# The value bias moved from GpSimd's additions to a row of the attention's value tail, with another order of prologue, loads and splits

## The chip, the cores and the metric

The kernel runs on one core of one Trainium2 chip. The metric is the device time of one execution in microseconds (us); smaller is better. The engines are TensorE (PE; PEld is its weight load), VectorE (DVE), ScalarE (ACT) and GpSimd (POOL). SyncE (SP) issues nearly all DMAs.

## The reference

A cross attention with layer norm and residual, and then a mixture of 16 experts and one shared expert, again with layer norm and residual, over x of 4 x 1024 x 256, a context of 4 x 154 x 256 and hidden size 128. Everything is fp32.

```python
q = einsum('bsd,de->bse', layernorm(x), Wq) + bq
k = einsum('bsd,de->bse', ctx, Wk) + bk
v = einsum('bsd,de->bse', ctx, Wv) + bv
scores = where(mask, q @ k.T / sqrt(256), -inf)
x = x + softmax(scores) @ v
...
xf = layernorm(x)
scores = sigmoid(l2norm(xf) @ l2norm(gate_w).T)
combine = top 8 of 16 scores, divided by their sum
routed = sum over e of combine_e * (silu(xf @ w_gate_e) * (xf @ w_up_e)) @ w_down_e
shared = silu(xf @ sw_gate) * (xf @ sw_up) @ sw_down
x = x + routed + shared
```

The sum of the softmax weights is one, so a bias on v reaches the attention's output as that same bias.

## The kernel before

The 4096 tokens are worked in 8 chunks of 512 (four tiles of 128; two halves q of two tiles each). Each chunk runs through 17 experts (expert 0 is the shared one), and in the places between experts the attention, layer norms and router of the next chunk are fitted in. The instructions of each engine stand in an order written by hand, and semaphores join the engines. The tables `PE_AT`, `ACT_AT`, `DVE_AT`, `POOL_AT`, `POOL_SOON` and `POOL_FIRST` say at which place s or s + .5 of the loop over experts a step of the next chunk (or, for SOON, of the chunk after it) stands.

TensorE works in three passes: each fp32 operand is split into a high and a low part, and high times high, high times low and low times high are summed (lines 393 to 395). For expert e of chunk c, written (c, e), the chain is: `gate` and `up` on PE (12 matmuls of 512 columns), `tanh_gate` on ACT (line 866), `silu_up` on DVE (lines 1145 and 1149), `weighted` on POOL (line 1351, times the routing weights in `cb`, or 1345 for the shared expert), `hidden_hi` on ACT (line 873), `hidden_lo` on DVE (line 1155), and `down` on PE (12 matmuls of 256 columns into y_ps). PE runs `gate` and `up` three experts ahead of `down`.

In chunk 0 the weights too are split, one expert at a time: a load of 384 KB into one of three staging places (`load_stage`), `split_hi` on ACT (line 795), and `split_lo` on DVE (line 999) or, for the experts in `POOL_SPLITS`, on POOL (line 1287). `load_stage(e)` waits for both splits of expert e - 3. In the loop, `split_hi(s + 5)` and `split_lo(s + 5)` stand ahead of `hidden_hi(c, s + 1)` and `hidden_lo(c, s + 1)` on their engines.

Of the 154 keys 128 are handled as one block, and 26 as a tail padded to 32 rows. The tail's values of all four batches come from one product (`value_tails`, line 484), are split into `vt`, and for batches 1 to 3 moved by nine DMAs to `Vtail` (`move_v_tails`, line 316). `ptail` holds the tails of the exponentials, `Vtail` those of the values, stacked as high, high and low in 96 rows; line 564 multiplies them. The exponentials are not normalised before: `residual` (line 1100) multiplies the product by 1 / esum and adds x. The bias bv is added to x by POOL (`add_bv`, line 1315, two instructions per chunk), and `residual` waits for it.

`mask_and_max` on DVE scales and masks the scores (line 1063), takes the maxima (1067) and negates them (1070), for the exponentials on ACT (`exps`, line 815). `add_bias` on POOL (line 1304) prepares the mask plus the query bias's part of the scores for a chunk. `write_t2_lo` (line 1050) makes the low part of the normalised tokens, for which `logits` on PE (line 575) waits.

## Time and profile before

| | us |
|---|---|
| Median of 3 runs | 651.84 |
| Lowest and highest run | 650.86, 651.99 |
| The profiled execution's own time | 650.85 |
| Its span, first to last instruction | 648.7 |
| PE busy in the span | 634.6 |
| DVE busy in the span | 472.7 |
| POOL busy in the span | 294.7 |
| ACT busy in the span | 235.7 |

The profile is one execution. PE busy counts matmuls that overlap at their ends once. What PE does not do in the span, 648.7 less 634.6, is 14.1 us. A timeline row gives the start of an instruction (or of a run of like ones, xN), how long it took, and in brackets how long its engine had been idle before it and what ended that.

### The profile page before, as it was taken

The numbers are of one execution on the slowest core, as the hardware profiler recorded it, in microseconds if no ns is written. First come the engines' busy times: TensorE is split into PE (matmuls) and PEld (weight loads), VectorE is DVE, ScalarE is ACT, GpSimd is POOL, SyncE is SP. The second block draws the span as 40 slices with busy tenths as digits, with TensorE's granted clock in tenths as the row PEclk, the third lists the DMA queues.
The fourth block names the chain that finished last, engine by engine and source line by source line (L and its number), as shares of the span: only waits on it lengthen the run. The fifth ranks groups of instructions, "written<-read, shape, count | busy, mean of one in ns | idle before, by whom it ended". The sixth has DMA issues, their size and how long they took to land.

```text
span 648.7 us, 10466 instructions
## 1 busy us (share of the span) xinstructions
PE 634.6 (98%) x3688; PEld 551.5 (85%) x3688; DVE 472.7 (73%) x941; ACT 235.7 (36%) x500; POOL 294.7 (45%) x275
## 2 busy tenths in 40 slices
PE   8898999999999999999999999999999999999997
PEld 7576888889888888888888898888888888888886
DVE  3779897868967588766868689675887768575443
ACT  5644444333243323433243332433234332432221
POOL 2517687333743356333563337433464334423333
PEclk9999899999999999999999999999999999999999
DMA  7265663424225324053244342263240531242100
GB/s 212 68 168 193 175 176 79 149 70 151 63 35 198 90 83 97 24 174 107 74 89 131 89 148 64 36 198 98 73 98 22 177 107 42 56 132 98 65 1 33
DMA packets 112655, 67.19 MB, mean 104 GB/s; under 512 B 80996, under 2 KB 102396, under 8 KB 112604
## 3 DMA queue, kind: packets, MB, share of 16 engines
q1 hardware_dynamic: 111516, 65.74, 36.0%
q10 hardware_dynamic: 1088, 0.79, 0.4%
q8 instruction: 30, 0.49, 0.3%
q14 instruction: 21, 0.17, 0.1%
HBM read 55.79 MB, written 10.42 MB: 102 GB/s over the span
## 4 chain that ended last, share of the span: by engine, by line
PE 91%; DVE 5%; issue 2%; ACT 1%; POOL 1%; POOLq 0%; ACTq 0%; DVEq 0%
PE y_ps L393 9%; PE gate_ps L395 9%; PE gate_ps L394 9%; PE up_ps L395 9%; PE up_ps L394 9%; PE gate_ps L393 9%; PE up_ps L393 9%; PE y_ps L394 9%; PE y_ps L395 9%; PE f_ps L538 2%; DVE hs L1155 1%; DVE W L999 1%; PE up_ps L402 1%; PE f_ps L575 1%; PE f_ps L393 1%
## 5 line engine op out<-in xcount | busy, mean ns | idle before, releaser
L1351 POOL TENSOR_TENSOR hidden<-hidden,cb 128x512 f32<-128x512 f32 x128 | 193.9, 1515 | 278.5 <-DVE hidden L1149 234.3
L866 ACT ACTIVATE hidden<-gate_ps 128x512 f32<-128x512 f32 x136 | 81.3, 598 | 292.9 <-PE gate_ps L395 292.9
L1145 DVE SCALAR_TENSOR_TENSOR hidden<-hidden,gate_ps 128x512 f32<-128x512 f32 x136 | 92.7, 681 | 102.9 <-ACT hidden L866 102.7
L393 PE MATMUL y_ps<-W,hs 128*128 128x256 f32 x544 | 154.7, 284 | 5.0 <-DVE hs L1155 5.0
L394 PE MATMUL y_ps<-W,hs 128*128 128x256 f32 x544 | 151.6, 279 | 0.0
L395 PE MATMUL y_ps<-W,hs 128*128 128x256 f32 x544 | 151.4, 278 | 0.0
L1155 DVE TENSOR_TENSOR hs<-hidden,hs 128x512 fp32r<-128x512 f32 x136 | 111.1, 817 | 21.8 <-ACT hs L873 21.6
L393 PEld LDWEIGHTS y_ps<-W,hs 128*128 128x128 f32 x544 | 102.2, 188 | 13.6 <-ACT hs L873 5.0
L393 PE MATMUL gate_ps<-xT,W 128*128 128x512 f32 x272 | 107.9, 397 | 0.0
L395 PE MATMUL gate_ps<-xT,W 128*128 128x512 f32 x272 | 107.6, 396 | 0.0
L394 PE MATMUL gate_ps<-xT,W 128*128 128x512 f32 x272 | 107.3, 395 | 0.0
L395 PE MATMUL up_ps<-xT,W 128*128 128x512 f32 x272 | 107.1, 394 | 0.0
L394 PE MATMUL up_ps<-xT,W 128*128 128x512 f32 x272 | 106.8, 393 | 0.0
L393 PE MATMUL up_ps<-xT,W 128*128 128x512 f32 x272 | 106.5, 392 | 0.0
L394 PEld LDWEIGHTS y_ps<-W,hs 128*128 128x128 f32 x544 | 102.7, 189 | 4.1
L1149 DVE TENSOR_TENSOR hidden<-hidden,up_ps 128x512 f32<-128x512 f32 x136 | 93.5, 688 | 12.5 <-PE up_ps L395 0.4
L395 PEld LDWEIGHTS y_ps<-W,hs 128*128 128x128 f32 x544 | 102.4, 188 | 0.0
L873 ACT ACTIVATE hs<-hidden 128x512 fp32r<-128x512 f32 x136 | 85.2, 626 | 44.2 <-POOL hidden L1351 42.1
L394 PEld LDWEIGHTS up_ps<-xT,W 128*128 128x128 f32 x272 | 51.2, 188 | 11.7
L393 PEld LDWEIGHTS up_ps<-xT,W 128*128 128x128 f32 x272 | 51.3, 188 | 11.6
L395 PEld LDWEIGHTS gate_ps<-xT,W 128*128 128x128 f32 x272 | 51.4, 189 | 10.9
L395 PEld LDWEIGHTS up_ps<-xT,W 128*128 128x128 f32 x272 | 51.3, 188 | 10.8
(162 smaller groups left out, 664.0 us busy)
## 6 DMA issues: line engine op xcount, KB each, us to landing
cb<-c_rows SPq DMA_DIRECT2D x64, 512.0 KB, 4.8
blocks<-in_x_dram SPq DMA_DIRECT2D x28, 128.0 KB, 2.9
xin<-in_x_dram SPq DMA_DIRECT2D x7, 512.0 KB, 4.1
t_rows<-blocks SPq DMA_DIRECT2D x28, 128.0 KB, 2.7
xs<-t_rows SPq DMA_DIRECT2D x7, 512.0 KB, 3.5
out_dram<-x SPq DMA_DIRECT2D x7, 512.0 KB, 6.2
p_rows<-blocks SPq DMA_DIRECT2D x28, 80.0 KB, 2.3
stage<-in_L_ffn_w_gate_dram SPq DMA_DIRECT2D x16, 128.0 KB, 2.5
```

Of the source, the lines that this page charges most:

```text
L393: mm(ps, lh, rh, start=first and i == 0, stop=False)
L394: mm(ps, lh, rl, start=False, stop=False)
L395: ins = mm(ps, ll, rh, start=False, stop=last and i == len(pairs) - 1)
L402: turn(up_ps[:, 0, 0:P], ident[:], ident[:])
L538: ins = mm(to, xs[:, k, j * P:(j + 1) * P], A[:, c // 2, k, :], start=k == 0, stop=k == KD - 1)
L575: mm(f_ps[0:2 * E, 0, :], G[:, k, :], xT[:, par, HI, k, :], start=k == 0, stop=False)
L866: af(ew[:, i, :], gate_ps[:, i, :], ACT.Tanh, scale=0.5).then_inc(tanh_done, 1)
L873: af(hs[:, i, HI, :], h[:, i, :], ACT.Copy).then_inc(h_hi, 1)
L1145: V_.scalar_tensor_tensor(out=ew[:, i, :], in0=ew[:, i, :], scalar=1.0, in1=gate_ps[:, i, :], op0=ALU.add, op1=ALU.mult).then_inc(silu_don ...
L1149: V_.tensor_tensor(ew[:, i, :], ew[:, i, :], up_ps[:, i, :], ALU.mult).then_inc(prod_done, 1)
L1155: V_.tensor_tensor(hs[:, i, LO, :], h[:, i, :], hs[:, i, HI, :].bitcast(F32), ALU.subtract) \
L1351: pg.tensor_tensor(h[:, i, :], ew[:, i, :], cb[:, pair % PLACES, (e - 1) % 2, :], ALU.mult) \
```

## The change

The bias of the values is no longer added to x. `bv_places` is a row of 128 zeros with a one at place 26 of each batch's 32, and one more matmul (one row deep, 256 columns) adds bv into row 26 of each batch's value tail in `value_tails`. ACT's exponentials put their sums no longer into `esum` of their own but into column 154 of `att`, so that the sum becomes row 26 of the exponentials' tail, and meets bv in the product of the tails: the output gets esum times bv, and bv after the division. `add_bv` and its 16 instructions on POOL are gone, with the 128 KB load for it.

The rest is order. The negation of the maxima is folded into the reduction. `add_bias` for the chunk after next goes from place 9.5 to 12.5. In the prologue both `exps` stand next to each other on ACT, the split of the tail values is divided, `router_scaled` and `turn_router` come later, `ln2(0, 1)` comes ahead of `ln2_scale(0, 0)`, and the loads of experts 3 and 4 and of the next chunk's x blocks go ahead of the nine tail DMAs, which go ahead of expert 5's load. In the loop the splits of weights stand behind `hidden_hi` and `hidden_lo`, and `split_lo(3)` ahead of the router. In the last chunk, `gate` and `up` of expert 16 come one `down` earlier.

```diff
-POOL_SOON = dict(add_bias=(9.5,), ln1_std=(11.5, 11.5), add_bv=(13.5, 14.5))
+POOL_SOON = dict(add_bias=(12.5,), ln1_std=(11.5, 11.5))
-POOL_FIRST = dict(ln1_std=(.5, .5), add_bv=(2.5, 4.5))
+POOL_FIRST = dict(ln1_std=(.5, .5))
-        bvb = sb("bvb", [P, D])
+        bv_row = sb("bv_row", [1, D])
+        bv_places = sb("bv_places", [1, B * PAD])
+        esum = att[:, :, KEYS]
...
@@ sync @@
-                sp.wait_ge(vt_split, 4)
+                sp.wait_ge(vt_split, 2)
...
+            sp.dma_start(bv_row[:], bv.partition_broadcast(1)).then_inc(bv_loaded, 16)
             sp.dma_start(wv_in, Wv.rearrange("(k p) e -> p k e", p=P)).then_inc(wv_loaded, 16)
             sp.dma_start(gw_in, gate_w).then_inc(gw_loaded, 16)
-            sp.dma_start(bvb[:], bv.partition_broadcast(P)).then_inc(bv_loaded, 16)
             for e in range(STAGES):
                 load_stage(e)
+            load_stage(STAGES)
+            load_stage(STAGES + 1)
+            load_x_blocks(1)
             move_v_tails()
-            for e in range(STAGES, STAGES + 3):
-                load_stage(e)
-            load_x_blocks(1)
             load_x(1)
+            load_stage(STAGES + 2)
             spread(0, 0)
...
@@ tensor @@
-                    ins = mm(y_ps[:, 0, D:2 * D], ctxTt[:, k, :], wv_in[:, k, :], start=k == 0, stop=k == KD - 1)
-                ins.then_inc(vt_made, 1)
+                    mm(y_ps[:, 0, D:2 * D], ctxTt[:, k, :], wv_in[:, k, :], start=k == 0, stop=False)
+                pe.wait_ge(bv_loaded, 16)
+                pe.wait_ge(pads_set, 2)
+                mm(y_ps[:, 0, D:2 * D], bv_places[:], bv_row[:], start=False, stop=True).then_inc(vt_made, 1)
...
             attend(0, 0)
-            turn_router()
             attend(0, 1)
             values(1, y_ps[:, 0, 0:D])
+            turn_router()
...
+                    if not ahead and s + AHEAD == NE - 1:
+                        gate(c, NE - 1)
+                        up(c, NE - 1)
                     down(c, s)
                     if ahead:
                         front(s, c + 1)
-                    if (s + AHEAD < NE or ahead) and not (c == 0 and s == 1):
+                    if (s + AHEAD < NE - 1 or ahead) and not (c == 0 and s == 1):
...
@@ scalar @@
                     af(att[:, j, 0:KEYS], att[:, j, 0:KEYS], ACT.Exp, bias=nmax[:, j:j + 1],
-                       accum_out=esum[:, j:j + 1]).then_inc(exped, 1)
+                       accum_out=att[:, j, KEYS:KEYS + 1]).then_inc(exped, 1)
...
             exps(0, 0)
-            write_vt_hi()
+            exps(0, 1)
+            vt_hi_first()
             write_v_hi(0, y_ps[:, 0, 0:D])
-            exps(0, 1)
             probs_hi_first(0)
             probs_hi_first(1)
+            write_vt_hi()
...
             write_v_hi(1, y_ps[:, 0, 0:D])
+            split_hi(3)
             bias_row_rest()
             router_hi()
-            split_hi(3)
+            split_hi(4)
             t2_hi_first(0)
             t2_hi_first(1)
             read_a_rest(0)
-            split_hi(4)
...
+                    if s + 1 < NE or ahead:
+                        hidden_hi(c, s + 1)
                     if c == 0 and s + EARLY < NE:
                         split_hi(s + EARLY)
-                    if s + 1 < NE or ahead:
-                        hidden_hi(c, s + 1)
...
@@ vector @@
-                V_.tensor_reduce(rsum[:, 2 * q:2 * q + 2], att[:, 2 * q:2 * q + 2, 0:KEYS], AX_X, ALU.max) \
-                    .then_inc(maxes, 1)
-                dve.wait_ge(maxes, upto(c, 2, q + 1))
-                V_.tensor_scalar(nmax[:, 2 * q:2 * q + 2], rsum[:, 2 * q:2 * q + 2], -1.0, None, ALU.mult) \
+                V_.tensor_reduce(nmax[:, 2 * q:2 * q + 2], att[:, 2 * q:2 * q + 2, 0:KEYS], AX_X, ALU.max, negate=True) \
                     .then_inc(maxed, 1)
...
-                dve.wait_ge(x_biased, upto(c, 2, q + 1))
...
             residual(0, 1)
+            ln2(0, 1)
             ln2_scale(0, 0)
-            ln2(0, 1)
             ln2_scale(0, 1)
...
             split_lo(2)
+            split_lo(3)
             sum_logits(0)
...
             hidden_lo(0, 0)
-            split_lo(3)
             write_v_lo(2, f_ps[:, 0, 0:D])
...
+                    if s + 1 < NE or ahead:
+                        hidden_lo(c, s + 1)
                     if c == 0 and s + EARLY < NE and s + EARLY not in POOL_SPLITS:
                         split_lo(s + EARLY)
-                    if s + 1 < NE or ahead:
-                        hidden_lo(c, s + 1)
...
@@ gpsimd @@
-                pg.memset(ident[:], 0.0).then_inc(pool_step, 1)
+                pg.memset(ident[:], 0.0)
+                pg.memset(bv_places[:], 0.0).then_inc(pool_step, 1)
...
-                pg.memset(att[:, :, KEYS:KROW], 0.0).then_inc(pads_set, 1)
+                pg.memset(att[:, :, KEYS + 1:KROW], 0.0).then_inc(pads_set, 1)
+                pg.memset(bv_places[:].rearrange("o (b r) -> o b r", r=PAD)[:, :, TAIL:TAIL + 1], 1.0).then_inc(pads_set, 1)
...
-            def add_bv(c, q):
-                if c == 0:
-                    pool.wait_ge(bv_loaded, 16)
-                    pool.wait_ge(t1_turned, q + 1)
-                pool.wait_ge(ln1_stats, upto(c, 2, q + 1))
-                xh = xin[:, 2 * q:2 * q + 2, :]
-                pg.tensor_tensor(xh, xh, bvb[:].unsqueeze(1).broadcast_to([P, 2, D]), ALU.add).then_inc(x_biased, 1)
```

DVE's order in the prologue, from the maxima of the first half to the tail probabilities of the first half, before (small is a tile with sums and maxima, zT here the router's weights):

```order
L1067 TENSOR_REDUCE small<-att 128x2
L1070 TENSOR_SCALAR small<-small 128x2
L1063 SCALAR_TENSOR_TENSOR att<-f_ps,small,keepb 128x154 x2
L1067 TENSOR_REDUCE small<-att 128x2
L1070 TENSOR_SCALAR small<-small 128x2
L983 TENSOR_SCALAR zT<-cb,gsq 16x256
L976 TENSOR_TENSOR Vtail<-y_ps,Vtail 32x256
L978 TENSOR_TENSOR vt<-y_ps,vt 128x256
L964 TENSOR_TENSOR V<-y_ps,V 128x256
L1076 RECIPROCAL small<-small 128x4
```

The same stretch in the changed kernel:

```order
L1085 TENSOR_REDUCE small<-att 128x2
L1081 SCALAR_TENSOR_TENSOR att<-f_ps,small,keepb 128x154 x2
L1085 TENSOR_REDUCE small<-att 128x2
L991 TENSOR_TENSOR Vtail<-y_ps,Vtail 32x256
L979 TENSOR_TENSOR V<-y_ps,V 128x256
L1090 RECIPROCAL small<-att 128x4
```

The two negations are gone, and the router's weights and the low part of vt have left this stretch for a place behind the tail probabilities.

DVE's order in chunk 0, from the low values of batch 3 to the low hidden part of expert 3, before (W<-stage is `split_lo`, hs<-hidden,hs is `hidden_lo`):

```order
L964 TENSOR_TENSOR V<-f_ps,V 128x256
L999 TENSOR_TENSOR W<-stage,W 128x768
L1155 TENSOR_TENSOR hs<-hidden,hs 128x512
...
L1063 SCALAR_TENSOR_TENSOR att<-f_ps,small,keepb 128x154 x2
L1067 TENSOR_REDUCE small<-att 128x2
L1070 TENSOR_SCALAR small<-small 128x2
L1145 SCALAR_TENSOR_TENSOR hidden<-hidden,gate_ps 128x512
L1149 TENSOR_TENSOR hidden<-hidden,up_ps 128x512
L999 TENSOR_TENSOR W<-stage,W 128x768
L1155 TENSOR_TENSOR hs<-hidden,hs 128x512
```

The same stretch in the changed kernel:

```order
L979 TENSOR_TENSOR V<-f_ps,V 128x256
L1168 TENSOR_TENSOR hs<-hidden,hs 128x512
L1017 TENSOR_TENSOR W<-stage,W 128x768
...
L1081 SCALAR_TENSOR_TENSOR att<-f_ps,small,keepb 128x154 x2
L1085 TENSOR_REDUCE small<-att 128x2
L1158 SCALAR_TENSOR_TENSOR hidden<-hidden,gate_ps 128x512
L1162 TENSOR_TENSOR hidden<-hidden,up_ps 128x512
L1168 TENSOR_TENSOR hs<-hidden,hs 128x512
L1017 TENSOR_TENSOR W<-stage,W 128x768
```

Each weight split now stands behind the hidden part that stood behind it, and the negation is gone.

POOL's order in the changed kernel in chunk 0 between the norms of the chunk after next and the shared expert of the next chunk:

```order
L1358 TENSOR_TENSOR hidden<-hidden,cb 128x512
L1320 TENSOR_TENSOR keepb<-keep,brow 128x616
L1358 TENSOR_TENSOR hidden<-hidden,cb 128x512 x3
L1352 TENSOR_SCALAR hidden<-hidden 128x512
L1358 TENSOR_TENSOR hidden<-hidden,cb 128x512 x8
```

Before, the same stretch had the two additions of bv and no keepb:

```order
L1351 TENSOR_TENSOR hidden<-hidden,cb 128x512 x2
L1315 TENSOR_TENSOR xin<-xin,bvb 128x512
L1351 TENSOR_TENSOR hidden<-hidden,cb 128x512
L1315 TENSOR_TENSOR xin<-xin,bvb 128x512
L1351 TENSOR_TENSOR hidden<-hidden,cb 128x512
L1345 TENSOR_SCALAR hidden<-hidden 128x512
L1351 TENSOR_TENSOR hidden<-hidden,cb 128x512 x8
```

keepb is `add_bias`; it now stands directly behind `weighted` of expert 13, and nothing else is left between the experts.

## Rows read from the trace of the kernel before

**Rows 1.** The page, part 1: busy time of each engine, share, instructions.

```profile
PE 634.6 (98%) x3688; PEld 551.5 (85%) x3688; DVE 472.7 (73%) x941; ACT 235.7 (36%) x500; POOL 294.7 (45%) x275
```

**Rows 2.** Timeline of PE: start, us, engine, line, operation; in brackets idle and releaser.

```profile
15.79 1.02 PE L484 MATMUL y_ps<-x,hidden 128*128 128x256 f32 x4
...
18.80 0.44 PE L545 MATMUL f_ps<-ident,att 128*128 128x128 f32 x2 [1.13 <-ACT att L815]
...
31.11 0.66 PE L508 MATMUL f_ps<-ident,xn 128*128 128x128 f32 x4 [1.06 <-DVE xn L1014]
...
33.92 0.62 PE L575 MATMUL f_ps<-xT,G 128*32 128x512 f32 x2 [0.61 <-issue]
...
56.92 0.35 PE L393 MATMUL y_ps<-W,hs 128*128 128x256 f32 x1 [1.01 <-DVE hs L1155]
...
63.44 0.36 PE L393 MATMUL y_ps<-W,hs 128*128 128x256 f32 x1 [2.06 <-DVE hs L1155]
...
96.96 0.36 PE L393 MATMUL y_ps<-W,hs 128*128 128x256 f32 x1 [0.89 <-DVE hs L1155]
```

**Rows 3.** Windows: the stretch 64 to 72 us; PEclk is the third from last.

```profile
64.00:72.00 8.00, 8.00 (x41) 6.87 (x40) 5.73 (x9) 1.85 (x3) 5.64 (x4) 0.79 0.74 191
```

**Rows 4.** Timeline of PE behind the longest gap, two neighbouring matmuls.

```profile
65.39 0.63 PE L394 MATMUL gate_ps<-xT,W 128*128 128x512 f32 x1
65.82 0.63 PE L395 MATMUL gate_ps<-xT,W 128*128 128x512 f32 x1
```

**Rows 5.** Timeline of DVE in the prologue, and one row of ACT.

```profile
15.70 0.47 DVE L1067 TENSOR_REDUCE small<-att 128x2 f32<-128x308 f32 x1
16.21 1.58 DVE L1070 TENSOR_SCALAR small<-small 128x2 f32<-128x2 f32 x1
...
30.32 0.73 DVE L1014 TENSOR_SCALAR xn<-x,meanvar,small 128x256 f32<-128x256 f32 x2 [1.11 <-POOL small L1295]
...
32.53 1.29 DVE L1044 TENSOR_TENSOR xT<-f_ps,xT 128x512 fp32r<-128x512 f32 x2 [1.05 <-ACT xT L804]
...
15.02 1.59 ACT L795 ACTIVATE W<-stage 128x768 fp32r<-128x768 f32 x2
```

**Rows 6.** Timeline of POOL: prologue, and the second expert of chunk 0.

```profile
15.96 3.58 POOL L1287 TENSOR_TENSOR W<-stage,W 128x768 fp32r<-128x768 f32 x2 [2.28 <-ACT W L795]
...
47.66 1.29 POOL L1351 TENSOR_TENSOR hidden<-hidden,cb 128x512 f32<-128x512 f32 x1 [5.33 <-DMA cb<-c_rows]
```

**Rows 7.** Timeline of DVE in chunk 0.

```profile
43.81 0.95 DVE L999 TENSOR_TENSOR W<-stage,W 128x768 fp32r<-128x768 f32 x1
...
51.37 1.78 DVE L1155 TENSOR_TENSOR hs<-hidden,hs 128x512 fp32r<-128x512 f32 x1
...
57.89 1.31 DVE L1070 TENSOR_SCALAR small<-small 128x2 f32<-128x2 f32 x1
...
60.93 1.75 DVE L999 TENSOR_TENSOR W<-stage,W 128x768 fp32r<-128x768 f32 x1 [0.42 <-ACT W L795]
```

**Rows 8.** Timeline of DVE and POOL before the gap at 96.96.

```profile
94.92 1.89 DVE L1155 TENSOR_TENSOR hs<-hidden,hs 128x512 fp32r<-128x512 f32 x1
...
94.87 1.39 POOL L1304 TENSOR_TENSOR keepb<-keep,brow 128x616 f32<-128x616 f32 x1
```

**Rows 9.** Timeline of DVE, POOL and PE around the router of a later chunk.

```profile
406.97 1.29 DVE L1050 TENSOR_TENSOR xT<-xs,xT 128x512 fp32r<-128x512 f32 x2 [1.02 <-ACT xT L810]
...
405.43 1.68 POOL L1351 TENSOR_TENSOR hidden<-hidden,cb 128x512 f32<-128x512 f32 x1 [0.32 <-DVE hidden L1149]
...
409.84 0.63 PE L575 MATMUL f_ps<-xT,G 128*32 128x512 f32 x2
```

**Rows 10.** Timeline of PE in the last chunk's end.

```profile
639.57 0.28 PE L393 MATMUL y_ps<-W,hs 128*128 128x256 f32 x1
639.69 0.28 PE L394 MATMUL y_ps<-W,hs 128*128 128x256 f32 x1
...
643.81 0.36 PE L393 MATMUL y_ps<-W,hs 128*128 128x256 f32 x1 [0.92 <-DVE hs L1155]
```

44 lines of the change are left out of this document (21 added, 23 removed).

## The prediction

> **What bounds the kernel now.** I read the busy times first. PE is busy in 634.6 of 648.7 us, DVE in 472.7, POOL in 294.7 [rows 1]: PE bounds the kernel, and all that a change of order can give back is what PE stands idle, or runs at a lower clock. So the second view is PE's timeline, read only for its bracketed waits. There are few, and nearly all lie in the first 100 us and in the last 10: 1.13 us at 18.80 for the exponentials, 1.06 at 31.11 for the second half of the normalised tokens, 0.61 at 33.92, 1.01 at 56.92, 2.06 at 63.44 and 0.89 at 96.96 for the low hidden part from DVE [rows 2], and 0.92 at 643.81 in the end [rows 10]. Between 97 and 641 us PE has no idle stretch worth a row; that part should only shift.
>
> The third view is the granted clock. In the windows from 64 to 72 us it is 0.79 on the mean [rows 3], directly behind the longest wait, and two neighbouring matmuls of 512 columns start 0.43 us apart there [rows 4]: 512 columns in 0.43 us is the lower level, 1.2 GHz. A mean of 0.79 over 8 us is 3.36 us at half speed, and costs 1.7 us.
>
> The fourth view is DVE's timeline in front of these waits: in chunk 0 it is DVE's queue, not PE's products, that is late.
>
> **The bias.** Added on PE: one product of 256 columns, one row deep. The two products of 256 columns of line 484 took 1.02 us [rows 2], so one costs at most 0.51 us; the floor is the 0.12 us by which `down`'s matmuls of that width, one pass each, start apart [rows 10]. I take 0.5, since it is plain fp32 as line 484 is. It falls in front of the wait of 1.13 us at 18.80, which hides it; it costs 0.5 if that cover is gone, and it will be, so I subtract it from what that wait gives.
> Two memsets on POOL are added, and only the first (128 elements) stands ahead of `ident`, for which PE's first work waits. The nearest row is `add_bias`, 616 elements a partition in 1.39 us [rows 8], so 128 cost at most 0.3; I put 0.1 us on the start, 0 to 0.3.
> Removed: 16 instructions of POOL and one load of 128 KB. POOL is no bound, so their own time brings nothing. They blocked DVE now and then; I count this below with `add_bias`.
>
> **The prologue.** DVE's maximum ends at 15.70 + 0.47 = 16.17, but the negation of two numbers behind it takes 1.58 us [rows 5], while POOL runs its weight splits from 15.96 [rows 6]. Folded in, the exponentials can start when ACT is through with its splits, at 15.02 + 1.59 = 16.61 [rows 5], 1.2 us earlier than 16.21 + 1.58 = 17.79. The exponentials' wait ended at 18.80, so they can now be ready at 17.6; PE is there at 17.67 (18.80 less 1.13), and with the new product at 18.17. So of 1.13 us 0.6 is gained. The second half of `exps`, now ahead of the value splits, is out of the way as well.
> `ln2(0, 1)` no longer waits behind `ln2_scale(0, 0)` on DVE. Before, that order put the second scaling at 30.32 behind 1.11 us of waiting for POOL [rows 5]. The statistics move ahead by the 0.73 us of a scaling and the wait in front of it, which with the shift before makes the second turn ready before PE comes. I count the whole 1.06.
> The wait of 0.61 at 33.92 ends with the low part of these tokens, 32.53 + 1.29 = 33.82 [rows 5], which is then early too; but the margin is a few tenths, so I count 0.5. `turn_router` no longer stands between the two `attend`s; 0.1. What queues behind: `values(1)` waits for vt's split, which moved behind the tail probabilities; PE gets to it after two `attend`s, so nothing. On SP the nine tail DMAs wait for the same split, and expert 5's load behind them is not needed until chunk 0's third expert.
> Prologue: 0.6 + 1.06 + 0.5 + 0.1 - 0.1 = 2.2 us.
>
> **The first experts.** DVE's stretch from 43.81 to the wait's end at 63.44 is full. Out of it go `split_lo(3)`, 0.95 us at 43.81 [rows 7], which now stands where DVE waits for the router; the negation of 1.31 us at 57.89, and its sister, which I count at nothing (0 to 1.58); and the split at 60.93, 1.75 us [rows 7], which now follows `hidden_lo(0, 3)` instead of preceding it. That is 0.95 + 1.31 + 1.75 = 4.0 us, against waits of 1.01 + 2.06 = 3.07 us. Both should go, with 0.9 us to spare, and with them the slow clock behind, 1.7 us. The prologue's 2.2 us must be carried by DVE too: it is, since its chain there starts with the router, behind the same PE products. One thing is not on DVE: `weighted(0, 1)` waited 5.33 us for the routing weights' transfer and started at 47.66 [rows 6]. The c_rows store behind it moves with PE, so it keeps its place.
> First experts: 1.0 + 2.1 + 1.7 = 4.8 us.
>
> **Chunk 0, expert 10.** The low hidden part at 94.92 took 1.89 us beside `add_bias` at 94.87, 1.39 us [rows 8]. Two like instructions together took 1.29 at 406.97 [rows 9], so 1.2 of the 1.89 was blocking. `add_bias` is gone from there; 1.2 exceeds the 0.89 of PE's wait. Gain 0.9.
>
> **Add_bias at 12.5.** It now starts when `weighted` of expert 13 ends, 405.43 + 1.68 = 407.11, and lasts 1.39 to 408.5. At 406.97 DVE begins the two instructions of `write_t2_lo`, 1.29 us, and `logits` on PE takes them at 409.84 [rows 9].
> At expert 10 the one instruction was blocked for about as long as the other ran (1.89 against 0.65, beside 1.39). If DVE is held until 408.5 here too, the low part is ready at 408.5 + 1.29 = 409.8, and PE wants it at 409.84. So it costs 0 if it just fits, and some 0.3 us if the hand-over adds to it, in six chunks: 0 to 1.8 us. Against it, the bv additions no longer block DVE near the router, worth 0 to 0.1 a chunk. I take 0 for both, and keep -0.7 to +1.8.
> By the Trainium skill's page "SBUF — State Buffer", section "Who interferes with whom", a DVE instruction with two SBUF inputs and a GpSimd one that reads SBUF exclude each other for a whole instruction, so the change moves a block onto the path to `logits`; the trace agrees in 1.89 against 0.65 us, and if both halves of `write_t2_lo` were blocked by that rule the sum would be rival 3's, not mine.
>
> **The end.** The last `down` starts at 643.81, and the one that was to cover its wait began at 639.57; matmuls start 0.12 us apart, twelve make 1.4 us [rows 10]. Two `down`s without waits would end at 642.4, so 1.4 us are lost. The chain from the last `up` to that `down` is 643.81 - 639.57 = 4.24 us, and three `down`s are 4.2: the last `up` ends 1.4 earlier, and the last `down` starts at about 642.5. Gain 1.3 (0.9 to 1.4).
>
> **Sum.** 2.2 + 4.8 + 0.9 + 1.3 = 9.2 us. On the profiled execution's own time, 650.85, that makes 641.65. It lies 1.0 us below the median of the runs shown, 651.84, and I forecast a median: 642.6.
>
> **Rivals.**
> 1. The forecast: the waits ahead of 100 us and the slow clock are gone, chance 0.56, 641 to 644.5.
> 2. DVE's queue in the first experts still ends late once. For it: the spare is 0.9 us on a stretch of 20, and a block such as the 1.78 us at 51.37 [rows 7] can fall on another instruction in the new order. Against it: each hidden part is now ahead of its split. A wait of 2.06 and the slow clock behind it, 1.7, come back: 642.6 + 3.8 = 646.4. Chance 0.25.
> 3. The block at `logits` costs its upper bound, 1.8: 644.4. Chance 0.08.
> 4. The early part is paced by the transfer of the routing weights, which lands as late as before because loads are issued earlier. The 5.33 us wait is for it. Then the prologue and the first experts give nothing, and PE's clock falls as before; the end and, if DVE is late elsewhere, only it remain: 651.84 - 1.3 = 650.5, no difference that counts. Against it: the store that the transfer waits for is itself behind the router. Chance 0.05.
> 5. Slower. The same block at `logits` in six chunks, but long enough that PE's clock falls each time, as behind the wait of 2.06: 6 x (2.06 + 1.7) = 22.6, so 642.6 + 22.6 = 665. It decides once PE loses more than 9.2 / 6 = 1.5 us in each. By the rows the low part would have to be 1.5 us later than 409.8, a second POOL instruction between its two halves. Chance 0.06.
>
> **The numbers.** What a measurement of this kernel can tell from no change is about 0.2%, 1.3 us. Faster by more: cases 1 to 3, 0.89. The same: case 4, 0.05. Slower: case 5, 0.06. The range from 640.8 (the steady part's 0.7 and the wider prologue) to 647.2 holds cases 1 to 3 but for their edges, about 0.84. Only case 5 has the other sign.
>
> **What would show it.** In the changed kernel's timeline of PE: the first turn of the exponentials starts at about 18.2, `logits` at about 31.7, no wait over 0.3 us before the third to sixth `down` of chunk 0, a granted clock of 1.00 from 56 to 72 us, none at expert 10, and the last `down` about 4.2 us behind the last `up`, with less than 0.2 us of idle time. The negations' absence shows as exponentials starting at 16.6. In later chunks `write_t2_lo` would take about 2.7 instead of 1.29 us; the chunk to chunk distance tells if that costs anything. I am wrong if a wait of a microsecond or more stays in front of a `down` in chunk 0, or if `logits` waits in each chunk.

## The result, and the profile after

The changed kernel takes 644.85 us in the median of five executions (644.41 to 645.24), against 651.99 (650.86 to 653.4) of the kernel before on the same chip: a ratio of 0.989, interval 0.987 to 0.9915. Measured again (below, e0_again) it was 0.993, interval 0.990 to 0.995. So it is faster by 0.7 to 1.1%. The profiled execution took 644.59 us, its span is 642.5; against 650.85 and 648.7 before that is 6.3 us less, where 9.2 were forecast.

The page, part 1, as in [rows 1]. PE is busy for 2.6 us less, though it has one more product. Its slow stretch is gone, which by the mean clock of 0.79 over 8 us [rows 3] is 1.7 of these:

```profile
PE 632.0 (98%) x3690; PEld 550.4 (86%) x3690; DVE 462.6 (72%) x925; ACT 235.8 (37%) x500; POOL 274.5 (43%) x261
```

PE's timeline, as in [rows 2], [rows 9] and [rows 10] (line 397 is the old 393, 582 the old 575): `logits`, `down` of expert 3 (at 63.44 in [rows 2]), the first `attend` for chunk 1, `down` of experts 8 and 10, `logits` of a later chunk, `down` of expert 15 in the last chunk.

```profile
31.56 0.63 PE L582 MATMUL f_ps<-xT,G 128*32 128x512 f32 x2
...
57.53 0.36 PE L397 MATMUL y_ps<-W,hs 128*128 128x256 f32 x1
...
71.39 0.36 PE L397 MATMUL f_ps<-V,xT 128*128 128x256 f32 x1 [1.09 <-DVE ptail L1096]
...
82.28 0.36 PE L397 MATMUL y_ps<-W,hs 128*128 128x256 f32 x1 [0.48 <-DVE hs L1168]
...
92.41 0.36 PE L397 MATMUL y_ps<-W,hs 128*128 128x256 f32 x1 [1.62 <-DVE hs L1168]
...
404.89 0.63 PE L582 MATMUL f_ps<-xT,G 128*32 128x512 f32 x2
...
636.20 0.36 PE L397 MATMUL y_ps<-W,hs 128*128 128x256 f32 x1 [0.24 <-DVE hs L1168]
```

The waits at 18.80, 31.11, 33.92, 56.92 and 63.44 are gone. But two new ones stand at 71.39 and 82.28, and the one of expert 10 has grown from 0.89 to 1.62. The window of [rows 3] now reads a granted clock of 1.00, with PE busy 6.91 of 8.00 because the wait at 71.39 lies in it:

```profile
64.00:72.00 8.00, 6.91 (x39) 5.70 (x38) 5.07 (x8) 4.29 (x8) 1.00 (x2) 1.00 0.71 205
```

Where the time went, by the starts of the first `down` matmul of an expert in both timelines: to expert 4 of chunk 0 (69.22 before, 61.78 after) 7.4 us are gained; from there to chunk 1's first `down` (127.47, 122.70) 2.7 are lost again; through chunks 1 to 6 (to 581.71, 576.57) 0.4 are gained, and in the last chunk to PE's last end (645.44, 639.18) 1.1. The forecast had 7.0, +0.9, 0 and 1.3. So one of its four parts is wrong, in sign too: the rest of chunk 0, where +0.9 was forecast and -2.7 came.

DVE's timeline in that part, from `hs` of expert 8 to that of expert 10, and POOL's beside it (L1168 is `hidden_lo`, L1017 `split_lo`, L1032 `ln2_scale`, L1056 `swap_x2`; POOL L1358 is `weighted`):

```profile
81.47 0.66 DVE L1168 TENSOR_TENSOR hs<-hidden,hs 128x512 fp32r<-128x512 f32 x1
...
83.37 1.33 DVE L1032 TENSOR_SCALAR xn<-x,meanvar,small 128x256 f32<-128x256 f32 x2
84.93 0.69 DVE L1168 TENSOR_TENSOR hs<-hidden,hs 128x512 fp32r<-128x512 f32 x1 [0.22 <-ACT hs L887]
85.66 0.96 DVE L1017 TENSOR_TENSOR W<-stage,W 128x768 fp32r<-128x768 f32 x1
86.54 1.70 DVE L1032 TENSOR_SCALAR xn<-x,meanvar,small 128x256 f32<-128x256 f32 x2
88.28 2.09 DVE L1056 STREAM_TRANSPOSE blocks<-xn 128x512 f32<-128x512 f32 x2
...
91.58 0.68 DVE L1168 TENSOR_TENSOR hs<-hidden,hs 128x512 fp32r<-128x512 f32 x1
...
82.94 1.29 POOL L1358 TENSOR_TENSOR hidden<-hidden,cb 128x512 f32<-128x512 f32 x1
...
86.49 1.28 POOL L1358 TENSOR_TENSOR hidden<-hidden,cb 128x512 f32<-128x512 f32 x1
```

As forecast, `hs` of expert 10 is no longer blocked: 0.68 us where [rows 8] has 1.89. Yet PE waits longer for it. Both scalings start within 0.5 us of a `weighted` on POOL, and last 1.33 and 1.70 us; the next experiments say why that is new.

In the steady chunks the block has moved onto `write_t2_lo` (L1068), beside `add_bias` (L1320), as [rows 9] had suggested it might: 2.51 us for the two instructions that took 1.29 there. It is so for four of the seven routed chunks; for chunks 1, 2 and 7 they still take 1.29.

```profile
401.95 2.51 DVE L1068 TENSOR_TENSOR xT<-xs,xT 128x512 fp32r<-128x512 f32 x2 [0.99 <-ACT xT L824]
...
402.08 1.84 POOL L1320 TENSOR_TENSOR keepb<-keep,brow 128x616 f32<-128x616 f32 x1
```

They end at 404.46, and `logits` starts at 404.89 without a wait: it just fits, and costs nothing there.

### The profile page after: what moved, and what is told of

It is laid out like the page before. It is cut to its first block, busy times and chain, and to the rows that moved or that the text cites. A ratio compares the mean times of both kernels' runs of the same rounds, so it can differ in the third digit from the quotient of the medians.

```text
span 642.5 us, 10415 instructions
## 1 busy us (share of the span) xinstructions
PE 632.0 (98%) x3690; PEld 550.4 (86%) x3690; DVE 462.6 (72%) x925; ACT 235.8 (37%) x500; POOL 274.5 (43%) x261
## 4 chain that ended last, share of the span: by engine, by line
PE 88%; DVE 3%; DMA 2%; issue 2%; POOL 2%; ACT 1%; SPq 1%; POOLq 0%; ACTq 0%; DVEq 0%
PE y_ps L397 9%; PE gate_ps L399 9%; PE up_ps L399 9%; PE y_ps L398 9%; PE gate_ps L398 9%; PE up_ps L398 9%; PE y_ps L399 9%; PE up_ps L397 9%; PE gate_ps L397 9%; PE f_ps L545 2%; POOL hidden L1358 1%; DMA cb<-c_rows 1%; PE f_ps L582 1%; DVE hs L1168 1%; PE f_ps L584 1%
## 5 line engine op out<-in xcount | busy, mean ns | idle before, releaser
L1358 POOL TENSOR_TENSOR hidden<-hidden,cb 128x512 f32<-128x512 f32 x128 | 193.0, 1509 | 281.3 <-DVE hidden L1162 237.7
L1168 DVE TENSOR_TENSOR hs<-hidden,hs 128x512 fp32r<-128x512 f32 x136 | 102.3, 752 | 25.5 <-ACT hs L887 25.0
```

Source lines behind the costliest of these rows:

```text
L1168: V_.tensor_tensor(hs[:, i, LO, :], h[:, i, :], hs[:, i, HI, :].bitcast(F32), ALU.subtract) \
L1358: pg.tensor_tensor(h[:, i, :], ew[:, i, :], cb[:, pair % PLACES, (e - 1) % 2, :], ALU.mult) \
```

## The experiments

The experiments are to decide between two theories. A: PE's new waits in chunk 0 have two causes, the transfer of the probabilities through memory, which is now what ends last at 71 us, and the new order of splits and hidden parts, which further on puts DVE's scalings beside POOL's products. B: they are DVE's full queue and nothing else, so that any order loses the same. In all runs but e8 the edit is made to the changed kernel. "To expert 4" and "to chunk 1" are the times at which PE starts `down` of expert 4 in chunk 0 and the first `down` of chunk 1, and "the end" is PE's last end. The prologue starts up to 0.4 us later in some profiles, when the load of the context lands late (a gap at 6.6 us); where that matters I compare with the profile that starts alike.

| run | median us | its ratio to before | to expert 4 | to chunk 1 | the end |
|---|---|---|---|---|---|
| before | 651.99 | 1 | 69.22 | 127.47 | 645.44 |
| changed | 644.85 | 0.989 (0.987 to 0.992) | 61.78 | 122.70 | 639.18 |
| e0_again | 646.82 | 0.993 (0.990 to 0.995) | 61.98 | 122.95 | 639.16 |
| e1_bias_at_9 | 647.30 | 0.991 (0.988 to 0.994) | 61.42 | 123.25 | 639.97 |
| e2_splits_ahead | 644.58 | 0.987 (0.984 to 0.990) | 62.69 | 125.24 | 642.27 |
| e3_end_back | 647.16 | 0.990 (0.987 to 0.993) | 61.79 | 122.57 | 640.53 |
| e4_probs_later | 646.49 | 0.989 (0.986 to 0.992) | 61.72 | 122.48 | 639.77 |
| e5_bias_at_13 | 645.03 | 0.991 (0.988 to 0.994) | 62.32 | 123.17 | 639.28 |
| e6_splits_and_13 | 643.92 | 0.988 (0.985 to 0.990) | 62.69 | 121.06 | 637.36 |
| e7_probs_first | 644.47 | 0.990 (0.987 to 0.992) | 61.65 | 121.51 | 638.80 |
| e8_bias_alone | 650.40 | 0.997 (0.995 to 0.999) | 65.87 | 125.32 | 642.62 |
| e9_negated_apart | 649.18 | 0.995 (0.993 to 0.997) | 63.63 | 127.45 | 643.92 |
| e10_prologue_order | 645.36 | 0.990 (0.987 to 0.993) | 62.29 | 123.42 | 640.46 |
| e11_mix | 645.02 | 0.988 (0.985 to 0.991) | 61.81 | 122.86 | 639.20 |

Each ratio is to executions of the kernel before that were taken beside it: their medians were 651.99 for the changed kernel, 652.92 for e1 to e4, 652.53 for e0 and e5 to e7, and 652.72 for e8 to e11. The intervals are 3 to 4 us wide and most overlap; what a single edit does is read from the timelines, each of which is one execution.

**The changed kernel again.**

> The changed kernel as it is, once more, on the same chip as the three that follow, so that they can be set against it. Every theory expects the waits of its first profile: about 1.1 us at the first attend of chunk 1 (71.4 us), 0.5 at down of expert 8, 1.6 at down of expert 10, none in the first experts, and a ratio of 0.986 to 0.992 to the kernel before. If a wait above 0.5 us is gone or new, the loss in chunk 0 is a matter of chance in when transfers land and not of the order.

PE waited 1.12 us at `attend`, 0.50 at expert 8, 1.56 at expert 10, and nowhere else from `logits` to the end of chunk 0 by 0.4 or more. The loss belongs to the order, not to chance. Its seven executions, though, went from 644.97 to 650.36 us.

**The bias row back at 9.5.**

```diff
-POOL_SOON = dict(add_bias=(12.5,), ln1_std=(11.5, 11.5))
+POOL_SOON = dict(add_bias=(9.5,), ln1_std=(11.5, 11.5))
```

> The changed kernel with one number put back: GpSimd's addition of the bias row at place 9.5 instead of 12.5. Theory A (the move frees the low hidden part of expert 10 and blocks the low part of the normalised tokens instead; both lie in slack from chunk 1 on): the two instructions of write_t2_lo together are 1.3 us again in every chunk, the low hidden part of expert 10 about 1.9 us, PE's wait there in chunk 0 grows from 1.62 to about 2.8 us, and chunks 1 to 6 stay as long as they are (within 0.3 us in all). Time 646.0. Theory B (the block at logits costs PE something in each chunk that only the removed bv additions made up for): chunks 1 to 6 become shorter by 0.2 us or more each, time 644 or less.

Theory A. In later chunks `write_t2_lo` is back at 1.29 to 1.35, and `hs` of expert 10 takes 1.41 where the changed kernel has 0.68:

```profile
91.29 1.41 DVE L1168 TENSOR_TENSOR hs<-hidden,hs 128x512 fp32r<-128x512 f32 x1
```
```profile
92.84 0.36 PE L397 MATMUL y_ps<-W,hs 128*128 128x256 f32 x1 [2.28 <-DVE hs L1168]
```

PE's wait is 2.28 instead of 1.62: moving `add_bias` is worth 0.7 us in chunk 0 (less than the 1.2 expected, since it blocks for a shorter time in this order). Chunks 1 to 6 take 454.13 us, against 453.87 and 453.60 in the two profiles of the changed kernel: the later place costs them nothing, and nothing is lost by the block at `logits`.

**The splits ahead of the hidden parts again.**

```diff
-                    if s + 1 < NE or ahead:
-                        hidden_lo(c, s + 1)
                     if c == 0 and s + EARLY < NE and s + EARLY not in POOL_SPLITS:
                         split_lo(s + EARLY)
+                    if s + 1 < NE or ahead:
+                        hidden_lo(c, s + 1)
```

and the same for `split_hi` and `hidden_hi` on ACT.

> The changed kernel with the weight splits of chunk 0 ahead of the hidden parts again, on ScalarE and VectorE, nothing else undone. Theory A (this order was what removed the waits ahead of the third and fourth down): a wait of 1 to 2 us comes back ahead of down of expert 3, the granted clock falls below 0.9 behind it, and down of expert 4 starts 2 to 4 us later than the 61.78 us of the changed kernel; of this some is given back at experts 5 and 10, whose waits shrink. Time 646 to 648. Theory B (the shorter queue alone, without the negations and with split 3 earlier, was enough): down of expert 4 starts within 0.5 us of 61.78, no change in the clock, time 644.5 to 645.2.

Both theories were off. Only 0.68 us of waiting came back ahead of expert 3, and the clock stayed at 1.00 there; expert 4 started 0.9 us later, 0.2 of them from the prologue. But the waits at experts 8 and 10 vanished, and the one of 1.09 at `attend` became one of 1.06 at `down` of expert 6 (the expectation of e6 puts it at `attend`). And at `logits` of chunk 1 this happened, in the timelines of DVE, POOL and PE:

```profile
99.91 3.51 DVE L1068 TENSOR_TENSOR xT<-xs,xT 128x512 fp32r<-128x512 f32 x2 [1.99 <-ACT xT L824]
...
99.79 1.30 POOL L1358 TENSOR_TENSOR hidden<-hidden,cb 128x512 f32<-128x512 f32 x1
101.03 1.84 POOL L1320 TENSOR_TENSOR keepb<-keep,brow 128x616 f32<-128x616 f32 x1
...
103.56 1.03 PE L582 MATMUL f_ps<-xT,G 128*32 128x512 f32 x2 [2.61 <-DVE xT L1068]
```

```profile
104.00:112.00 8.00, 8.00 (x38) 6.34 (x37) 3.68 (x9) 3.52 (x11) 2.95 (x2) 0.86 0.01 2
```

That is rival 5's mechanism, once: `write_t2_lo` is blocked by `weighted` and by `add_bias` one behind the other, `logits` waits for 2.61 us, and the clock falls to its lower level behind it. Two things lead to it: PE is not held up at expert 10, and the tokens' transfer lands late (ACT's copy starts at 99.25, in e6 at 98.05), so that the low part is not through when `weighted` begins. It happened in the profiled execution, 647.69 us; the other three took 644.02 to 644.62. (A wait of 0.60 at `logits` at 332.39 is only late tokens: there the low part took 1.29.)

**The end as before.** `gate` and `up` of the last expert go behind `down` of expert 13 again.

```diff
-                    if not ahead and s + AHEAD == NE - 1:
-                        gate(c, NE - 1)
-                        up(c, NE - 1)
                     down(c, s)
```

> The changed kernel with the last expert's gate and up behind down of expert 13 of the last chunk, as before. Theory A (the end gained 1.0 us by it): the wait ahead of the last down becomes 0.9 to 1.3 us, the last down starts 1.0 us later against down of expert 0 of that chunk, time 645.9. Theory B (the end's gain came from somewhere else, such as a queue that runs emptier): less than 0.3 us.

Theory A: the last `down` waits for 0.88 us again, as in [rows 10], and from the last chunk's first `down` to the last one it is 62.11 us instead of 61.09. So this edit is worth 1.0.

```profile
638.91 0.36 PE L397 MATMUL y_ps<-W,hs 128*128 128x256 f32 x1 [0.88 <-DVE hs L1164]
```

**The probabilities' parts behind the hidden part.**

```diff
-probs_hi=(5,) ... probs_lo=(5,)
+probs_hi=(5.5,) ... probs_lo=(5.5,)
```

> The changed kernel with the high and low parts of the probabilities at place 5.5 instead of 5, so that on ScalarE and VectorE the hidden part of expert 6 stands ahead of them. It tells what makes PE lose 2.7 us in the rest of chunk 0. Theory A (the wait for the transfer of the probabilities blocks both engines in their order, and the lost time is what queues behind): the wait of 1.09 us at 71.39 stays or grows by at most 0.7 us, since the transfer lands when it did, but those behind it (0.48 at 82.28, 1.62 at 92.41) shrink by 0.5 us or more together. Theory B (the waits at experts 8 and 10 come from VectorE's own queue at places 7 to 9 and have nothing to do with the transfer): they stay within 0.2 us. In chunks 1 to 6 no theory expects more than 0.1 us each. Time A 644.3, B 645.3.

Neither quite: 1.41 us at `attend`, none at expert 8, 1.93 at expert 10, 3.3 in all against 3.2. A wait taken away at one place came back at the next.

**The bias row at 13.5**, the first edit of e1 with 13.5.

> GpSimd's addition of the bias row one place later still, 13.5, where VectorE has no instruction with two SBUF inputs beside it. Theory A (the block of write_t2_lo is hidden by slack, except in an execution where the tokens' transfer lands late): write_t2_lo takes 1.3 instead of 2.5 us in every chunk, the low hidden part of expert 15 stays at 0.69, chunks 1 to 6 are as long as they were (0 to 0.3 us shorter in all), the time is within 0.5 us of the unchanged one. Theory B (the block costs something in each chunk, through the tanh and router chain behind it): each of chunks 1 to 6 0.1 us or more shorter, time at least 0.7 us less.

Theory A. `write_t2_lo` took 1.29 to 1.36 us in every chunk, and chunks 1 to 6 453.50 us against 453.60 of e0_again: the block cost nothing there.

**Splits ahead and the bias row at 13.5**, both edits together.

> The weight splits of chunk 0 ahead of the hidden parts again, and the bias row at 13.5. With the splits ahead and the bias row at 12.5 PE waited 0.68 us at expert 3, 1.07 at attend, nothing at experts 8 and 10, and 2.61 at logits of chunk 1, where write_t2_lo took 3.51 us beside GpSimd's product and bias row. Theory A (those 2.61 us are the block of write_t2_lo, and nothing else): they shrink to 0.5 us or less, the clock stays at 1.00 there, and with 1.8 us of waits in chunk 0 against 3.2 of the changed kernel the time is 1.0 to 1.5 us below it. Theory B (PE comes to logits before the tokens' transfer has landed and been split, whatever GpSimd does): a wait of 1 us or more stays, time within 0.5 us of the changed kernel.

The time is theory A's: no wait at `logits`, and only 0.68 at expert 3 and 1.06 at expert 6 stay. But the cause is not shown by this run, since the tokens' transfer also landed 1.2 us earlier than in e2: the low part started at 98.71 instead of 99.91 and was through at 100.03, when `weighted` had just begun (99.96). The last end is 1.8 us earlier than in the changed kernel. Against e5 only the order of splits and hidden parts differs: all four executions (643.47 to 644.16) are below all six of e5 (644.24 to 649.68), and chunk 1 starts 2.1 us earlier, though expert 4 starts 0.4 later. DVE's timeline for the same work as above:

```profile
81.32 0.66 DVE L1168 TENSOR_TENSOR hs<-hidden,hs 128x512 fp32r<-128x512 f32 x1
...
83.63 0.93 DVE L1032 TENSOR_SCALAR xn<-x,meanvar,small 128x256 f32<-128x256 f32 x2
84.48 0.95 DVE L1017 TENSOR_TENSOR W<-stage,W 128x768 fp32r<-128x768 f32 x1
85.35 0.68 DVE L1168 TENSOR_TENSOR hs<-hidden,hs 128x512 fp32r<-128x512 f32 x1
85.95 0.73 DVE L1032 TENSOR_SCALAR xn<-x,meanvar,small 128x256 f32<-128x256 f32 x2
86.72 2.12 DVE L1056 STREAM_TRANSPOSE blocks<-xn 128x512 f32<-128x512 f32 x2
...
90.05 0.69 DVE L1168 TENSOR_TENSOR hs<-hidden,hs 128x512 fp32r<-128x512 f32 x1
```

```profile
86.90 1.30 POOL L1358 TENSOR_TENSOR hidden<-hidden,cb 128x512 f32<-128x512 f32 x1
```

Instruction by instruction: the second scaling takes 0.73 instead of 1.70, since it is through at 86.68, before `weighted` starts at 86.90; the first takes 0.93 instead of 1.33; and the split fills the time in which DVE idles for 0.22 us. That is 0.97 + 0.40 + 0.22 = 1.6 us, less 0.2 for an idle stretch that e6 has at 82.22: from the start of `hs` of expert 8 to that of expert 10 it is 8.73 us instead of 10.11. `hs` of expert 10 ends at 90.74 instead of 92.26. This is nearly all of the wait of 1.62.

**The probabilities' transfer first on SP.**

```diff
-            load_stage(EARLY + 5)
             store_probs(1)
-            load_stage(EARLY + 6)
             load_probs(1)
+            load_stage(EARLY + 5)
+            load_stage(EARLY + 6)
```

> The changed kernel with the store and the load of chunk 1's probabilities ahead of the loads of experts 10 and 11 on SP. Theory A (the round trip of the probabilities is what PE waits for at 71.39, and what ScalarE, VectorE and GpSimd stand behind): the store begins 0.4 us earlier and the load no longer shares the queue with a weight load, so it lands about 1.5 us earlier, the wait of 1.09 us at attend goes to 0.2 or less, and the waits behind it (0.48 and 1.62) shrink by 0.3 us or more. Theory B (the waits at experts 8 and 10 are VectorE's own queue at places 7 to 9): PE comes there 1.1 us earlier and they grow by as much, so the time is unchanged. If the weights of experts 10 and 11 come late instead, a wait for a split shows at gate of expert 10 or 11.

Theory A for `attend`: ACT's copy of the landed probabilities starts at 66.90 instead of 68.00, and the wait is gone. Those at experts 8 and 10 are as long as before (0.50 and 1.65), though PE and DVE both come there 1.1 us earlier. I read that so: DVE's chain to these experts starts at `attend`, as PE's does, so its length counts, not when it starts. Chunk 1 starts 1.2 us earlier; 0.67 us of it was lost again at 328.81, at `logits`, where the tokens' transfer landed late.

```profile
68.00 0.63 ACT L842 ACTIVATE xT<-xn 128x512 fp32r<-128x512 f32 x1 [2.60 <-DMA xn<-p_rows]
```
```profile
66.90 0.63 ACT L842 ACTIVATE xT<-xn 128x512 fp32r<-128x512 f32 x1 [1.69 <-DMA xn<-p_rows]
```

(the first fence is the changed kernel's timeline of ACT, the second that of e7).

**The value bias alone.** The kernel before, with nothing but the bias's part of the change (the product on PE, the sums in `att`, `add_bv` removed).

```diff
-POOL_SOON = dict(add_bias=(9.5,), ln1_std=(11.5, 11.5), add_bv=(13.5, 14.5))
-POOL_FIRST = dict(ln1_std=(.5, .5), add_bv=(2.5, 4.5))
+POOL_SOON = dict(add_bias=(9.5,), ln1_std=(11.5, 11.5))
+POOL_FIRST = dict(ln1_std=(.5, .5))
...
+                mm(y_ps[:, 0, D:2 * D], bv_places[:], bv_row[:], start=False, stop=True).then_inc(vt_made, 1)
```

> The kernel before with the value bias's row alone: the product of one row behind the two of the tails (line 484), the sums written into the attention's tail, GpSimd's additions of bv gone, its row loaded ahead of Wv. All orders, the negation, the bias row's place 9.5 and the end are those of before. Theory A (the bias change by itself is worth nothing: its product of about 0.6 us lies in front of the wait for the exponentials, and GpSimd is no bound): the wait at 18.80 shrinks by 0.5 us, logits starts within 0.3 us of 33.92, the waits of the first experts, of expert 10 and of the end stay within 0.3 us, time within 0.7 us of the kernel before. Theory B (GpSimd's additions had blocked VectorE in the first experts): the waits of 1.01 and 2.06 us at experts 2 and 3 shrink by 1 us or more together, the clock behind stays at 1.00, time 2 to 4 us less.

In its times theory B, against what I had forecast. The ratio is 0.997, below 1 with its whole interval, and PE's last end is 2.8 us earlier; this is the profile of the fastest of ten executions (648.04; median 650.40 against 652.72, 2.3 less). The prologue is longer by 0.4 us (below); but the first experts have one wait of 0.98 us instead of 1.01 and 2.06, and the clock behind it stays at 1.00. To expert 4 3.4 us are gained, of which 1.2 are lost again before chunk 1, 1.06 of them in a new wait at expert 6. DVE's timeline shows where the gain is from:

```profile
51.80 0.69 DVE L1159 TENSOR_TENSOR hs<-hidden,hs 128x512 fp32r<-128x512 f32 x1
...
53.60 0.17 DVE L1075 TENSOR_SCALAR small<-small 128x2 f32<-128x2 f32 x1
...
57.16 0.17 DVE L1075 TENSOR_SCALAR small<-small 128x2 f32<-128x2 f32 x1
...
60.76 0.68 DVE L1159 TENSOR_TENSOR hs<-hidden,hs 128x512 fp32r<-128x512 f32 x1
```

The negation that took 1.31 us at 57.89 [rows 7] takes 0.17. In the timeline of before this stood beside it on POOL, `add_bv` for chunk 1:

```profile
57.88 1.29 POOL L1315 TENSOR_TENSOR xin<-xin,bvb 128x512 f32<-128x512 f32 x1
```

The other negation takes 0.17 instead of 0.60, and `hs` of expert 1 0.69 instead of the 1.78 of [rows 7]. Together that is 2.7 us less on DVE, of which 0.4 is lost at another `hs`. But only the first, 1.14 us, stood beside an addition. `hs` of expert 1 is free because `weighted` of expert 2 now starts at 52.41, when it is nearly through (51.05 before): the routing weights landed later (`weighted` of expert 1 at 48.44 instead of 47.66), and a small instruction of POOL in between took 1.28 instead of 0.70. The smaller negation had stood beside a split. These two are shifts between the engines, not blocks by `add_bv`, and whether they would come again is not shown. Chunks 1 to 6 take 453.58 us instead of 454.24, 0.1 each.

**The negation apart.**

```diff
-                V_.tensor_reduce(nmax[...], att[...], AX_X, ALU.max, negate=True).then_inc(maxed, 1)
+                V_.tensor_reduce(rsum[...], att[...], AX_X, ALU.max).then_inc(maxes, 1)
+                dve.wait_ge(maxes, upto(c, 2, q + 1))
+                V_.tensor_scalar(nmax[...], rsum[...], -1.0, None, ALU.mult).then_inc(maxed, 1)
```

> The changed kernel with the negation of the maxima as an instruction of its own again, in all chunks. Theory A (it stood under GpSimd's splits in the prologue and in the first experts): the exponentials start 0.8 to 1.2 us later than 16.58, PE waits 0.5 to 1.0 us at the first turn of the exponentials, and in the first experts, where the low hidden part of expert 3 has 0.15 us to spare and that of expert 4 0.28, a wait of 0.5 to 1.3 us appears at down of expert 3 or 4. Down of expert 4 starts 1 to 2.5 us later than in the changed kernel; the rest of chunk 0 gives back up to 1 us. Theory B (elsewhere the two numbers cost 0.1 us each and the splits have moved): under 0.4 us in all.

Theory A in the prologue, B behind it. In the prologue the negation takes 1.58 us under POOL's split, as in [rows 5], and the exponentials wait 1.21 for it:

```profile
16.72 1.58 DVE L1088 TENSOR_SCALAR small<-small 128x2 f32<-128x2 f32 x1
```
```profile
18.33 0.42 ACT L829 ACTIVATE att<-att,small 128x154 f32<-128x154 f32 x1 [1.21 <-DVE small L1088]
```

`logits` starts at 33.33, 1.4 us later than in the profile of the changed kernel that starts alike (31.95). From there to expert 4 it is 30.3 us against 30.0: with `add_bv` gone, the negations take 0.73 and 0.62 and cost 0.3. But then `attend` waits for 2.76 us, since the probabilities landed late, and the clock falls behind it:

```profile
74.91 0.36 PE L397 MATMUL f_ps<-V,xT 128*128 128x256 f32 x1 [2.76 <-DVE ptail L1100]
```
```profile
76.00:80.00 4.00, 4.00 (x22) 4.00 (x22) 2.43 (x5) 1.37 (x2) 3.66 (x3) 0.57 0.39 107
```

Its ten executions took 647.39 to 651.85 us, the ten of e10 and e11, measured beside it, 642.21 to 646.12. So the folding is worth more than the 1.7 us that the timeline shows to expert 4. In the profiled execution the rest is the longer wait at `attend` and the slow clock; in four executions the mean clock was 1.00 (647.39 to 648.90), and what they lost beyond the 1.7 is not known.

**The order in the prologue.**

```diff
             residual(0, 1)
-            ln2(0, 1)
             ln2_scale(0, 0)
+            ln2(0, 1)
             ln2_scale(0, 1)
```

> The changed kernel with the first scaling of the normalised tokens of chunk 0 ahead of the second half's statistics again, on VectorE. Theory A (this order was the wait of 1.06 us in front of the second turn): a wait of 0.5 to 1.1 us comes back there, logits starts 0.5 to 1.1 us later than 31.6 to 31.9, and the whole is later by as much less what the following waits give back. Theory B (the second turn was early because the chain had moved by the exponentials): less than 0.2 us.

Theory A: the wait of [rows 2] at 31.11 is back, and `logits` starts at 32.22, 0.8 us later than in e1, whose prologue starts alike (31.41).

```profile
30.10 0.65 PE L515 MATMUL f_ps<-ident,xn 128*128 128x128 f32 x4 [0.97 <-DVE xn L1032]
```

**The mixture.** The edits of e5 and e7, and in the loops of ACT and DVE:

```diff
+                    if c == 0 and 6 <= s < NE - EARLY and s + EARLY not in POOL_SPLITS:
+                        split_lo(s + EARLY)
                     if s + 1 < NE or ahead:
                         hidden_lo(c, s + 1)
-                    if c == 0 and s + EARLY < NE and s + EARLY not in POOL_SPLITS:
+                    if c == 0 and s < 6 and s + EARLY not in POOL_SPLITS:
                         split_lo(s + EARLY)
```

> A mixture: the changed kernel with the bias row at 13.5, the probabilities' store and load ahead of the loads of experts 10 and 11, and the splits of chunk 0 behind the hidden parts up to place 5, ahead of them from place 6. Theory A (the waits at experts 8 and 10 come from the order of split and hidden part at places 8 and 9, where the scalings run into GpSimd's products; the one at attend from the transfer): no wait above 0.5 us between 33 and 600 us, chunk 1's first down at 119.6 to 120.5 (122.70 in the changed kernel, 121.06 with the splits ahead everywhere), time 2 to 3 us below the changed kernel. Theory B (VectorE's queue at places 7 to 9 is simply full, and the order only helped because PE came later): PE comes to expert 10 a microsecond earlier than with the splits ahead everywhere, and a wait of 1 us stays there; chunk 1's first down at 121 or later.

As theory A has it, the waits at experts 8 and 10 are gone as such: what is left there are gaps between matmuls of 0.1 to 0.3 us. But the sum fails, and chunk 1 starts at 122.86, not at 119.6 to 120.5: the probabilities' first load started at 65.85 instead of e7's 63.89, because their store had landed later, `attend` waited for 1.89 us, and `logits` for 0.73. This last wait tells of the bias row's place what e6 could not. The low part starts at 99.91 as in e2, with `weighted` beside it at 100.46 but no `add_bias` behind, and it takes 2.39 us instead of 3.51:

```profile
99.91 2.39 DVE L1070 TENSOR_TENSOR xT<-xs,xT 128x512 fp32r<-128x512 f32 x2 [1.31 <-ACT xT L824]
```

Of all kernels here e6 has the lowest median; by the ratios e2 (0.987), e6 and e11 (0.988) cannot be told apart.

## Why the prediction was right and wrong

**The time and the direction.** 642.6 was forecast, 640.8 to 647.2; it is 644.85. That is in the range, but just outside the likeliest case's own 641 to 644.5. The measured time lies near rival 3's 644.4, but that is chance: nothing was lost at `logits` in this profile, and no rival as told came true. By the prediction's own sign it was wrong ("a wait of a microsecond or more stays in front of a `down` in chunk 0"): at expert 10 there is one of 1.62. The range held because it was wide enough for 2.7 us lost in the rest of chunk 0.

**Prologue, 2.2.** Right in size: `logits` moved from 33.92 to 31.56, 2.4 us. By single edits, the negation is worth 1.4 up to `logits` rather than 0.6, and the order of `ln2` 0.8 rather than 1.06. The new product took 0.62 us of PE (L492 starts at 16.83, the next at 17.45), where I had put 0.5 and called 0.51 the most. One thing I had not priced: the loads of experts 3 and 4. ACT waits for expert 3's weights in front of its copy of the tokens, in the kernel before and, longer, in e8 (the two rows in this order):

```profile
31.17 0.84 ACT L795 ACTIVATE W<-stage 128x768 fp32r<-128x768 f32 x1 [2.44 <-DMA stage<-in_L_ffn_w_down_dram]
...
31.62 0.84 ACT L800 ACTIVATE W<-stage 128x768 fp32r<-128x768 f32 x1 [3.21 <-DMA stage<-in_L_ffn_w_down_dram]
```

SP issued that load at 27.65 and 27.89, behind nine tail DMAs; in the changed kernel at 17.96. While ACT is held until about 32 us, the low part is not ready before 33.82 [rows 5], however early the rest comes. So by these rows nearly all of the gain at `logits` hangs on that move, for which the sum had no term: that it came out right is luck. Undoing the move alone was not tried.

**First experts, 4.8.** Right in size: 7.4 us to expert 4 with the prologue, 7.0 forecast, and the clock held. Wrong in the source. "The negation of 1.31 us at 57.89" was counted for the folding; it was blocked by `add_bv`, and e8 frees it without folding. I had counted the blocks by `add_bv` near the router only, at 0 to 0.1 a chunk; there it is 0.1, but in the first experts more. From `logits` to expert 4 it takes 35.3 us before, 31.5 with the bias alone (e8) and 30.2 in the changed kernel: by these profiles the bias's edit alone gives 3.8 of the 5.1 us, in part by a shift between the engines and not by the additions it removes (e8). The order of split and hidden part, which I gave 1.75 of the 4.0 us, is worth 0.7 there (e2), and the folding 0.3 (e9). That the sum was right with its terms so placed is luck.

**Expert 10, 0.9.** The step that failed. The block of 1.2 us did go, and e1 shows that this is worth 0.7. But the step took the rest of chunk 0 as it was, while the loop's new order holds for all of chunk 0, not for the first experts alone. At places 8 and 9 it delays the scalings into `weighted` on POOL: 1.4 us on `hs` of expert 10, shown by e6 against e5, which differ in this order alone, and again by e11. The reorder is thus worth 0.7 in front and costs more behind: chunk 1 starts 2.1 us earlier without it, and the median is 1.1 lower. And the first experts' gain made `attend` the next to wait. Before, the low part of the probabilities was through at 75.92, 1.5 us ahead of PE at 77.47:

```profile
75.24 0.68 DVE L1082 TENSOR_TENSOR ptail<-xn,ptail 32x512 fp32r<-32x512 f32 x1
...
77.47 0.28 PE L393 MATMUL f_ps<-V,xT 128*128 128x256 f32 x1
```

Now it comes 4.7 us earlier, and PE 7.2. With a gain of 7 us in the sum, I did not ask which transfer would come less than 7 us earlier. e7 shows 1.1 us for it.

**Add_bias at 12.5, 0.** Right for the steady chunks (e1, e5). The low part took 2.5 us and ended at 404.46; I had 2.7, and nothing lost "if it just fits". In chunk 0 there is less to spare: where the wait at expert 10 is gone and the tokens' transfer lands late, the block struck once (e2), at 2.6 us and a slow clock. The Trainium skill, "SBUF — State Buffer", section "Who interferes with whom", says that a DVE instruction with two SBUF inputs and a GpSimd one that reads SBUF contend for a port that one of them holds exclusively; the traces agree in 2.51 and 3.51 against 1.29 us for `write_t2_lo`. I had looked for such blocks only in rivals 3 and 5; they should have been looked for at every DVE instruction that the reorder shifts. The scalings (L1032), with one tensor from SBUF and two scalars per partition, are held too: 1.33 and 1.70 against 0.73 us.

**The end, 1.3.** Right in mechanism, and a little smaller: 1.0 by e3; 0.24 us of waiting is left one `down` earlier, at expert 15.

**What stays open.** How much of the 0.5% and more by which executions of one kernel differ is due to transfers that land late was not measured, only seen in profiles. Not undone by themselves were the loads' new place, `split_lo(3)` ahead of the router, and the later `turn_router` and `router_scaled`. What the folding is worth beyond the 1.7 us to expert 4 (e9) is open. Why `hs` of expert 3 starts 0.3 to 0.6 us behind ACT's copy in some profiles was not looked into.

## What to carry to other kernels

When an instruction of a fifth of a microsecond takes 1.3, look for what ran beside it before giving the gain to whoever removes it: two edits that both free it count once. And look whether the two only happen to meet: a shift of half a microsecond between the engines frees or blocks it as well. A reorder inside a loop is priced at every place that the loop reaches, not only where the stall is; and after a gain of some microseconds, list what was early by less than that, transfers first. A cover that is itself a stall (PE late at expert 10) shrinks once the stall is mended.
